# Routing logits as half-precision products, a split of the attention outputs, and a new instruction order in a one-core attention and mixture-of-experts kernel

## What is computed

```python
x = x + xattn(layernorm(x), ctx, ctx)
x = x + ffn(layernorm(x), gate_w, gate_b, w1, b1, w2, b2)

# xattn: 16 x 256 tokens, D = 256 = 16 heads x 16; attention is across the 16 heads of one token
scores = einsum('bsqd,bskd->bsqk', qh, kh) / sqrt(16)   # causal over the heads
out    = einsum('bsqk,bskd->bsqd', softmax(scores), vh)

# ffn: 8 experts, hidden size 1024
logits = xf @ gate_w.T + gate_b
top1   = argmax(logits)
out    = relu(xf @ w1[e].T + b1[e]) @ w2[e].T + b2[e]    # e = top1 of the token
```

## Time and profile before

| | us |
|---|---|
| three executions | 471.26, 469.33, 470.85 |
| median | 470.85 |
| span of the profiled execution, first to last instruction | 462.9 |
| PE busy | 384.6 (83%) |
| DVE busy | 339.8 (73%) |
| POOL busy | 207.6 (45%) |
| ACT busy | 181.1 (39%) |

### The profile page before, as it was taken

How to read it: one execution, slowest core, us unless ns; L and a number is a source line. 1 busy time by engine, 2 the same in 40 slices (tenths; PEclk the granted TensorE clock), 3 DMA queues, 4 the chain that set the end, 5 groups by cost and what they waited for, 6 DMA issues and landing times.

```text
span 462.9 us, 16301 instructions
## 1 busy us (share of the span) xinstructions
PE 384.6 (83%) x5889; PEld 328.5 (71%) x5889; DVE 339.8 (73%) x777; ACT 181.1 (39%) x317; POOL 207.6 (45%) x213
## 2 busy tenths in 40 slices
PE   0126878996798969895699999898999999999991
PEld 0026767996698869894688877676788888787870
DVE  8789799789882875378676987596867677766761
ACT  2344446454542523143353433243443434434320
POOL 8536444635673548643342354743333233233321
PEclk9999999955555555565589999999999999999998
DMA  7999989889778675667552544757543443434310
GB/s 264 417 254 236 264 220 260 260 188 240 200 161 218 159 160 112 180 141 219 125 143 67 107 98 106 186 139 184 106 94 99 95 108 90 104 84 106 100 29 0
DMA packets 125802, 73.17 MB, mean 158 GB/s; under 512 B 99229, under 2 KB 110238, under 8 KB 125216
## 3 DMA queue, kind: packets, MB, share of 16 engines
q1 hardware_dynamic: 96336, 60.46, 50.6%
q0 software_dynamic: 3408, 8.46, 5.0%
q10 hardware_dynamic: 25984, 3.21, 4.9%
HBM read 48.28 MB, written 11.24 MB: 129 GB/s over the span
## 4 chain that ended last, share of the span: by engine, by line
PE 58%; DVE 12%; issue 8%; SPq 7%; POOL 6%; DMA 5%; ACT 2%; POOLq 0%; DVEq 0%; ACTq 0%
PE s_ps L1506 19%; PE at_ps L1522 7%; PE pv_ps L1522 6%; PE s_ps L1403 6%; PE pv_ps L1433 5%; PE lg_ps L1459 4%; DMA arena<-qv_hl 3%; PE at_ps L1523 3%; PE pv_ps L1523 3%; SPq L601 3%; PE tr_ps L1445 2%; DVE arena L1186 2%; PE at_ps L1420 2%; POOL sorted_rows L1340 1%; POOL qv_hl L1296 1%
## 5 line engine op out<-in xcount | busy, mean ns | idle before, releaser
L1506 PEld LDWEIGHTS s_ps<-arena 128*128 x1872 | 131.9, 99 | 43.4 <-issue 4.9
L1506 PE MATMUL s_ps<-arena 128*128 128x128 f16 x1872 | 157.0, 221 | 2.8 <-issue 1.2
L1203 DVE SCALAR_TENSOR_TENSOR arena<-arena,s_ps 128x512 f32<-128x512 f32 x78 | 53.5, 685 | 32.5 <-PE s_ps L1506 21.1
L1433 PE MATMUL pv_ps<-a_hl,arena 128*128 128x16 f16 x1536 | 54.6, 180 | 17.1 <-DMA arena<-qv_hl 12.3
L1433 PEld LDWEIGHTS pv_ps<-a_hl,arena 128*128 128x128 f16 x1536 | 53.3, 118 | 20.7 <-DMA arena<-qv_hl 16.7
L1366 POOL DMA_INDIRECT result<-arena x39 | 38.9, 996 | 64.4 <-DVE arena L1228 60.3
L1403 PEld LDWEIGHTS s_ps<-k_hl,arena 128*128 128x128 f16 x1536 | 54.5, 118 | 15.4 <-DMA arena<-qv_hl 10.6
L1522 PE MATMUL at_ps<-arena,k_in 128*128 x160 | 60.3, 379 | 2.8 <-DVE k_hl L1214 2.8
L1359 POOL TENSOR_TENSOR arena<-arena 128x256 f32<-128x256 f32 x39 | 29.5, 756 | 73.4 <-DMA arena<-b 73.3
L1403 PE MATMUL s_ps<-k_hl,arena 128*128 128x16 f16 x1536 | 54.2, 180 | 9.7 <-DMA arena<-qv_hl 9.7
L1522 PE MATMUL pv_ps<-arena,x_in 128*128 x152 | 57.6, 379 | 0.0
(11 more groups left out here) (141 smaller groups left out, 589.9 us busy)
## 6 DMA issues: line engine op xcount, KB each, us to landing
arena<-w SPq DMA_DIRECT2D x28, 512.0 KB, 5.1
arena<-sorted_rows SPq DMA_DIRECT2D x39, 130.0 KB, 2.2
arena<-b SPq DMA_DIRECT2D x39, 128.0 KB
arena<-qv_hl SPq DMA_DIRECT2D x70, 64.0 KB
k_in<-k_t SPq DMA_DIRECT2D x16, 256.0 KB
arena<-x SPq DMA_DIRECT2D x4, 1024.0 KB, 10.6
x_in<-x_t SPq DMA_DIRECT2D x16, 256.0 KB, 5.0
v_in<-v_t SPq DMA_DIRECT2D x16, 256.0 KB
```

Of the source, the lines that this page charges most:

```text
L1203: eng.scalar_tensor_tensor(out=h_in[:, c].rearrange("p (k t) -> p k t", t=P), in0=bias, scalar=W_SCALE, in1=h_ps[c][:].rearrange("p (k t) ...
L1433: m = eng.matmul(o[:, n], v_bd[i][:, n // 2, :, n % 2, v], a_hl[:, n, a, :], start=(n, a, v) == (0, 0, 0), stop=(n, v) == (BLK - 1, 1))
L1506: k = eng.matmul(o, weights_of(j, w + k_ * H + n * P, P), xt[:, j % XB, a + k_], start=(k_, w, a) == (0, HI_1, 0), stop=k_ == KD - 1 and w ...
```

## The change

- The logits: `o_sb` is split into `o_hl` (ACT copies the high part, POOL subtracts for the low part, per chunk), `gate_w` times 64 into `gate_hl` (two small DVE instructions), and `gate_bd` now holds both halves, made by two POOL products of 1024 columns (`gate_blocks`) where DVE made it in one. A step of `gates` is 12 half-precision products of 64 columns (three for each of four heads) where it was 4 float32 ones. `o_hl` is laid out so that 32 tokens of one head lie next to each other, 4 bytes apart; `o_sb` is read 16 elements apart for it. The logits are divided by 64 where DVE scales them.
- `load_residual` waits for the two halves of the chunk four before, where it waited for the group's logits.
- `sel` is made by a product of two views of `turn_of` instead of a copy.
- The scratch space of GpSimd's own transfers is 2048 bytes a partition; it was the default of 16384.
- Every number of `TIMES` is new, so each engine's order is another.

```diff
-        gate_bd = sb("gate_bd", [P, HEADS, 8, E])
+        gate_bd = sb("gate_bd", [P, HEADS, 2, 8, E], F16)
+        gate_hl = sb("gate_hl", [P, 2, HEADS * E], F16)
...
+        o_hl = sb("o_hl", [P, HEADS, P, 2], F16)
...
             def load_residual():
...
-                    sp.wait_ge(s_logits, i // CG)
+                    sp.wait_ge(s_o_hi, i - CG + 1)
+                    sp.wait_ge(s_o_lo, i - CG + 1)
...
+            def output_halves():
+                for i in range(NC):
+                    at = slice(i % CG * BLK, (i % CG + 1) * BLK)
+                    yield
+                    act.wait_ge(s_o, i + 1)
+                    act.wait_ge(s_logits, i // CG)
+                    eng.copy(o_hl[:, :, at, 0], o_sb[:, at, :].rearrange("p t h -> p h t")).then_inc(s_o_hi, 1)
...
-                eng.tensor_copy(sel[:], turn_of[:].unsqueeze(2).to_broadcast([P, 8, HD])).then_inc(s_select, 1)
+                eng.tensor_tensor(sel[:], turn_of[:].unsqueeze(2).to_broadcast([P, 8, HD]),
+                                  turn_of[:].unsqueeze(2).to_broadcast([P, 8, HD]), ALU.mult).then_inc(s_select, 1)
...
-                eng.tensor_tensor(gate_bd[:], ...
+                eng.tensor_scalar(gate_hl[:, 0], gate_sb, W_SCALE, None, ALU.mult).then_inc(s_gate_hl, 1)
+                dve.wait_ge(s_gate_hl, 1)
+                eng.scalar_tensor_tensor(out=gate_hl[:, 1], in0=gate_sb, scalar=W_SCALE, in1=gate_hl[:, 0], op0=ALU.mult,
+                                         op1=ALU.subtract).then_inc(s_gate_hl, 1)
...
+            def gate_blocks():
+                yield
+                pool.wait_ge(s_select, 3)
+                pool.wait_ge(s_gate_hl, 2)
+                for n in range(2):
+                    eng.tensor_tensor(gate_bd[:, :, n], ..., ALU.mult).then_inc(s_gate_bd, 1)
+
+            def output_halves():
...
+                    pool.wait_ge(s_o_hi, i + 1)
+                    eng.tensor_tensor(lo, o_sb[:, at, :].rearrange("p t h -> p h t"), hi, ALU.subtract).then_inc(s_o_lo, 1)
...
-                            pe.wait_ge(s_o, CG * (g + 1))
+                            pe.wait_ge(s_o_hi, CG * (g + 1))
+                            pe.wait_ge(s_o_lo, CG * (g + 1))
...
-                            m = eng.matmul(LG, o_sb[:, :, h], gate_bd[:, h].rearrange("p b e -> p (b e)"), start=h == 0,
-                                           stop=h == HEADS - 1)
+                            for a, w in ((0, 0), (0, 1), (1, 0)):
+                                m = eng.matmul(LG, o_hl[:, h, :, a], gate_bd[:, h, w].rearrange("p b e -> p (b e)"),
+                                               start=(h, a, w) == (0, 0, 0), stop=(h, a) == (HEADS - 1, 1))
...
-    nc = bacc.Bacc("TRN2", target_bir_lowering=False, num_devices=1)
+    nc = bacc.Bacc("TRN2", target_bir_lowering=False, num_devices=1, dynamic_dma_scratch_size=2048)
```

Of the table one lane shows the kind of edit, PE's `gates` (four steps and a rank step for each group):

```diff
         "gates": (
-            8153, 8500, 8991, 9201, 10701, 12450, 12621, 12706, 13577, 16137, 16863, 17034, 17119, 18125, 20196,
-            20742, 21081, 21361, 22026, 26084
+            8840, 8894, 9065, 9589, 10626, 14084, 14926, 14980, 15034, 16050, 19353, 19407, 19461,
+            19515, 20354, 21339, 21393, 21579, 21633, 25736
         ),
```

More of the change, by code:

```diff
@@ L97 @@
[L97 to L103 removed]
[4 rows of a table removed]
+            1632, 3901, 5169, 6261, 7253, 8533, 9555, 10727, 11871, 13050, 14246, 15197, 16188, 17694,
+            18710, 19540
@@ L130 @@
     "DVE": {
-        "constants": (170, 509, 1405, 2045, 4500),
+        "constants": (0, 340, 1526, 1606, 4348),
         "statistics": (
[5 rows of a table removed]
[5 rows of a table added]
+        ),
+        "spreads": (1183, 4690, 9088, 13487),
+        "queries": (
+            1357, 1432, 1546, 1872, 2465, 2608, 3374, 3468, 5040, 5115, 5309, 5599, 6383, 6505, 7376,
+            7450, 9335, 9410, 9843, 9964, 10211, 11199, 12267, 12706, 13668, 13743, 14328, 14448, 14695,
+            14770, 15815, 16125
+        ),
+        "softmax": (
[6 rows of a table added]
+        ),
@@ L138 @@
+        "outputs": (
+            4931, 5506, 7180, 7659, 9675, 10315, 11064, 12208, 14542, 15360, 15612, 16598, 19222, 19287,
+            20579, 20819
+        ),
+        "layer_norms": (
[6 rows of a table added]
+        ),
+        "choose": (
[5 rows of a table added]
+        ),
+        "counts": (25791,),
+        "plans": (
[5 rows of a table added]
         ),
         "weights": (
[5 rows of a table removed]
-        ),
-        "spreads": (1615, 4826, 9226, 13513),
[5 rows of a table added]
+        ),
+        "expert_inputs": (
[3 rows of a table added]
+        ),
+        "hiddens": (
[6 rows of a table added]
+        ),
+        "rests": (
[6 rows of a table added]
+        ),
+        "results": (
[6 rows of a table added]
+        ),
+    },
@@ L147 @@
+    "POOL": {
+        "constants": (0, 189, 292),
+        "zeros": (382, 1131),
+        "statistics": (967, 2357, 4884, 9350),
         "queries": (
-            1735, 1800, 1923, 2180, 2870, 3047, 3595, 3718, 5310, 5375, 5793, 5947, 6988, 7052, 7111, 7415,
-            9395, 9512, 9840, 9910, 10595, 10973, 11424, 12161, 13738, 13802, 14287, 14453, 14800, 15354, 16254,
-            16621
-        ),
-        "softmax": (
[6 rows of a table removed]
+            1591, 2522, 2805, 4116, 5384, 6058, 7302, 7610, 9569, 10254, 11408, 13135, 13931, 15054,
+            15579, 16943
+        ),
+        "keys": (
+            1918, 2934, 4468, 5063, 5934, 7187, 8748, 9736, 10513, 11667, 12959, 14173, 14929, 16079,
+            17718, 18388
+        ),
+        "values": (
+            1720, 3986, 5254, 6346, 7431, 8619, 9851, 10812, 12053, 13370, 14331, 15282, 16274, 17834,
+            18795, 19625
+        ),
+        "weights_of_softmax": (
+            3180, 4362, 5776, 6783, 7881, 8864, 10149, 10984, 12183, 13264, 14710, 15713, 17072, 18092,
+            19120, 20052
+        ),
+        "tables": (59,),
+        "gate_blocks": (3332,),
+        "output_halves": (
+            6476, 6960, 7751, 8169, 10383, 10629, 11537, 12829, 15819, 15949, 18198, 18925, 19922,
+            20273, 21070, 21200
+        ),
+        "layer_norms": (9981, 15412, 19755, 24561),
+        "row_tails": (162, 15183, 18328, 22676),
+        "scatters": (
+            11138, 11273, 11783, 11918, 12289, 12424, 12559, 12694, 16403, 16538, 16673, 16808, 17178,
+            17313, 17448, 17583, 20530, 20665, 20800, 20935, 21330, 21465, 21600, 21735, 26348, 26483,
+            26690, 26960, 27095, 27230, 27436, 27706
+        ),
+        "skipped_rows": (23785,),
+        "residuals": (
[3 rows of a table added]
+        ),
+        "stores": (
[3 rows of a table added]
+        ),
+    },
@@ L159 @@
+    "PE": {
+        "statistics": (1239, 4922, 9144, 13550),
+        "gate_columns": (1324,),
+        "scores": (
+            1367, 3427, 4563, 5486, 6496, 7510, 9229, 9959, 11044, 12383, 13724, 14480, 15513, 16578,
+            17754, 18591
+        ),
+        "turned": (
+            3341, 4477, 5890, 6944, 8178, 8979, 10319, 11404, 12298, 13379, 14840, 15873, 17187, 18245,
+            19267, 20167
         ),
         "outputs": (
-            5246, 6929, 7474, 7751, 10069, 11032, 11817, 12326, 14571, 15283, 16563, 16680, 19068, 19573, 20571,
@@ L256 @@
[L256 to L269 removed]
+            3901, 5169, 6179, 7193, 8523, 9643, 10727, 11871, 12948, 14164, 15197, 16261, 17437, 18950,
@@ L888, in _ @@
             weave(TIMES["ACT"], spread_first_queries=spread_first_queries(), spread=spread(), queries=queries(),
-                  keys=keys(), values=values(), turned_rows=turned_rows(), exponentials=exponentials(),
+                  keys=keys(), values=values(), turned_rows=turned_rows(), output_halves=output_halves(),
+                  exponentials=exponentials(),
                   weights=weights(), expert_inputs=expert_inputs(), relus=relus())
```

178 lines of the change are left out of this document (64 added, 114 removed), and 289 rows, old and new, of the table TIMES.

## The result

The change took **479.38 us** (median of 4, 478.23 to 481.28) beside 471.06 us for the kernel before on the same chip: ratio 1.0208, 95% interval 1.0159 to 1.0258. It is slower by 2%, where 450.4 us was forecast. The profiled execution has a span of 476.5 us.

A forecast was written before the change was run, and what follows sets the result against it. PE was taken to bound the experts' stage, and a ring of short steps with no engine full to bound attention. Terms summed to -20.5 us, from 470.85 to 450.4 us; forecast band 443 to 457 (0.68), range 442 to 463.

The forecast's parts named there:

- the term of the split: Attention: added casts on ACT and subtractions on POOL mostly fit their idle time; +2 us, bounds 0 and +8.
- the order's term: All queues: a new order moves a little of PE's waiting for diagonal transfers; -2 us, bounds -6 and +6.
- Logits' products: PE in attention: 192 half-precision products replace 128 fp32 records, mostly gained on the path; -14.5 us, bounds -3.5 and -19.
- Rival B: Attention: diagonal transfers take up PE's relief beyond 10 us; 461 us, sign over 35 us of waiting, chance 0.13.
- `sel`, -2.5: Start: a product frees 4.8 us over the copy, but first chunks also await transfers; -2.5 us, bounds 0 and -4.8.
- `gate_bd`, 0: After chunk 0's softmax weights: POOL's two products, 5.5 us together, covered by idle time; 0, bounds -0.8 and +5.5.
- VectorE against GpSimd: Attention: a new order avoids shared-port collisions; -3.5 us, bounds -9 and +2.3; the cited rule could give 456 us.
- Rival A: Split's strided reads of `o_sb` slow casts and subtractions, POOL holds up scores; term near +11, 459 to 460 us, chance 0.14.
- C: POOL's scatters wait several us each on the smaller scratch; 495 us, chance 0.05 shared with other losses.

The follow-up runs named there:

- e1: The kernel before with only GpSimd's transfer scratch cut to 2048 bytes, also called the base: 464.83 us, ratio 0.9858 to the kernel before.
- e3: The change's arithmetic with the order of the kernel before: 475.80 us, ratio 1.0122 to the kernel before.
- e5: e1 with 12 of every 16 fp32 logits products left out and nothing in their place: 459.71 us, ratio 0.9794 to the kernel before.
- e2: The kernel before with only `sel` made by a product instead of a copy: 470.48 us, ratio 0.9984.
- e12: e3 without POOL's 16 subtractions, the high half taken twice, still 192 products: 465.61 us, ratio 0.9893 to the kernel before.
- e18: e6 with POOL's 16 subtractions replaced by memsets of an unread buffer: 474.61 us, ratio 1.0207 to the kernel before.
- e6: e1 with the outputs' split made on ACT and POOL but read by nothing, products still fp32: 480.72 us, ratio 1.0241 to the kernel before.
- e7: e6 with ACT's 16 casts alone, no subtractions on POOL: 465.69 us, ratio 0.9901 to the kernel before.
- e9: e1 with its own arithmetic in the change's order, with a second output buffer: 483.80 us, ratio 1.0309 to the kernel before.
- e14: e9 with the change's order only up to the table's 180 us, the old order after: 476.61 us, ratio 1.0148 to the kernel before.
- e15: e9 with the old order up to the table's 180 us, the change's order after: 480.04 us, ratio 1.0219 to the kernel before.

## Why the prediction was wrong

Its view of the kernel held: a ring of short steps in attention, the experts' stage full of PE. It then added terms as if each engine's idle time were free cover, in a ring where idle time is each engine's wait for the others. The step that failed is the term of the split, below; the order's term failed beside it.

- **Logits' products, -14.5.** The size on PE was right: 15.6 us forecast, 14.6 measured (386.9 to 372.3, e1 and e3), and 58 ns for one of 192. Its worth on the path was wrong. 18 us off PE gave 5 (e5), a quarter, so this relief is worth about -4. That a step outside the chain "delays what stands behind it in a strict queue" failed: behind it PE then waited longer for the diagonal transfers (13.7 to 20.2 us) and for `pay` (1.2 to 6.9). Rival B named the first of these waits; it gave even this too much, 10 us. Its sign, over 35 us, was set on the earlier trace rows, which counts PE and its weight loads both.
- **`sel`, -2.5.** It fell from 5.11 to 0.28 us, and the product that needs it (L1387) came at 13.74 us in e2 instead of 16.02, 2.3 us earlier and not 4.8; worth nothing in the time (e2). That is the 0 of the bounds, for which the forecast had named the transfers; which wait takes it up was not followed.
- **`gate_bd`, 0.** 3.8 us on POOL, cheaper than forecast. In the old order the high half alone, with `gate_bd` on POOL, is level with the base (e12), so something eats up the relief of some 4 us. PE's wait for the casts ahead of the products, 9.4 us for 2.8, is a candidate beside `gate_bd`; they were not tried apart.
- **VectorE against GpSimd, -3.5.** L1220's mean is 838 ns against 871, 1.8 us in all, and small routing steps pay it back, such as the one of 1.44 us; how much of PE's 14.1 us of waiting for `seen` is theirs wasn't measured. The rule cited (the Trainium skill, SBUF — State Buffer, Who interferes with whom) is borne out by 1.44 us for a product of 64 columns beside POOL's subtractions, 0.21 without. But the time that it gave, 456, is not: e18 shows that what the subtractions hold up on DVE is the small part of what they cost.
- **The split, +2.** The term that failed most. It is +15 to +16 on the base (e6), twice the upper bound of 8. The casts are free (e7), as argued; "Their cover is POOL's 107 us and ACT's 136 us of idle time" is wrong for POOL: its steps behind a subtraction, softmax weights and scatters, come later by its length, and with them PE's work and the next writing of `pay`. Rival A had the mechanism nearly, POOL as what the ring waits for, but hung it on the stride. The stride is worth little: in e6 the subtractions took 1586 ns in the mean beside 1365 for the queries', a sixth more (a fifth by the medians, 1544 and 1286). The rule cited for A (the Trainium skill, GPSIMD Engine Reference, Performance pitfalls for Q7 kernels), about half more over 8 bytes, is more than this trace shows.
- **The order, -2, bounds -6 to +6.** +19 with the old arithmetic (e9), +3.6 in the change. The bounds were drawn from the one wait that a better order might shorten. With the old arithmetic every departure from the old table, also by half (e14, e15), lost 11 us or more; but only one other order was tried, and why the old one is better stays open but for the end of attention.
- **The scratch**, which had no term and a rival on the slow side (C), gave 4.3 us. C's sign, scatters of several us, did not come.

Sum as measured: scratch -4.3, relief -3 to -4, split +15, order +3.6 on top: some +11 against the 8.3 measured; as the table of orders shows, the parts don't add, so it is no exact account.

## To carry to other kernels

In a ring of short steps through strict queues, an engine at half busy is no cover. Here 25 us of steps added to POOL cost 15, and 18 taken from PE gave 5: price an added step at more than half of its duration, and one taken away at a fraction, until a run with the step made and read by nothing says otherwise. The order is a part of the tuning like any other: run the new arithmetic in the old order and the old arithmetic in the new before both are judged together. Look behind the last store. And where a view gives PE and its weight loads together, read PE's waits alone.

## What the hardware showed that was not expected

- POOL's closing drain depends on the scratch of its transfers: 7.06 us with the default (7.07 in e2), 2.78 to 2.79 with 2048 in every other trace.
- Beside scatters back to back (one in 1.28 us) PE's products came in pieces of 4 or 5, one piece in 0.74 to 0.85 us (e15 and the change), and of one to three in e9, waiting for nothing that the profile shows ("issue").
- A cast with reads 64 bytes apart took ACT 1094 ns for 512 columns, where casts of neighbours took 787.
- In e9 the granted clock was 1.00 from 100 to 150 us, where it was 0.50 in e1, and the kernel still took 19 us longer. Why it was granted longer was not settled.
